# Five weight products of a four-layer graph network, by quarters in Strassen's seven products

## The reference

```python
# layer 0: x1 = x @ W1 + b1; four gate steps of _graph_gcn (tanh of two gate projections per edge)
# layer 1 (sage), twice: 
h = relu(x @ W_self0 + (agg(x) * deg_inv) @ W_neigh0 + b0)
out = h @ W_self1 + (agg(h) * deg_inv) @ W_neigh1 + b1
# layer 2 (attention): h = x @ W; e = exp(-leaky(al[src] + ar[dst])); elu(segment_sum(e * h[dst]) / rowsum)
# layer 3 (loop): relu(segment_sum((x @ W)[src] * norm) + b)
x = _layernorm(x + layer(x, ...))
```

## Time and profile before

| | us |
|---|---|
| median of three executions | 1535.95 (1535.74 to 1536.42) |
| span of the profiled execution | 1534.3 |
| TensorE busy | 1515.2 |
| VectorE busy | 883.6 |
| ScalarE busy | 753.9 |
| GpSimd busy | 187.2 |
| DMA moved | 231.75 MB, 151 GB/s on average |

### The profile page before, as it was taken

The page is one execution under the profiler, slowest core; times in us unless marked ns, Lnnn a source line. Parts: engine busy times, 40 slices in busy tenths (PEclk is TensorE's granted clock), DMA queues, the critical chain, the costliest instruction groups (busy, mean ns, idle before and its releaser), DMA issues.

```text
span 1534.3 us, 19219 instructions
## 1 busy us (share of the span) xinstructions
PE 1515.2 (99%) x6985; PEld 1220.1 (80%) x6985; DVE 883.6 (58%) x1410; ACT 753.9 (49%) x1348; POOL 187.2 (12%) x307
## 2 busy tenths in 40 slices
PE   7999999999999999999999999999999999999997
PEld 6887877878887887788878777888888778877776
DVE  9888788887545442423332353567598356436346
ACT  7677767768633342433332233345696246533233
POOL 0110021333200000000000000212053013100003
PEclk9999999999999999999999999999999999999999
DMA  6333154226764424333354424554466248545336
GB/s 200 123 122 107 47 191 132 84 78 224 261 237 149 161 96 155 119 113 116 114 171 130 143 81 166 196 203 166 147 197 190 94 143 297 182 131 171 94 121 186
DMA packets 103198, 231.75 MB, mean 151 GB/s; under 512 B 23162, under 2 KB 25972, under 8 KB 103096
## 3 DMA queue, kind: packets, MB, share of 16 engines
q1 hardware_dynamic: 90126, 191.62, 39.3%
q10 hardware_dynamic: 12970, 38.77, 6.6%
HBM read 170.98 MB, written 59.37 MB: 150 GB/s over the span
## 4 chain that ended last, share of the span: by engine, by line
PE 96%; DVE 3%; ACT 1%; issue 0%; DMA 0%; POOLq 0%; DVEq 0%; ACTq 0%
PE bank L986 18%; PE bank L842 16%; PE bank L844 15%; PE bank L843 15%; PE bank L997 9%; PE bank L990 9%; PE bank L988 9%; PE bank L1075 2%; PE bank L912 2%; PE bank L880 1%; DVE oK L1801 0%; ACT Tt L1159 0%; DVE wl L1445 0%; DVE Tt L1483 0%; DVE oL L1791 0%
## 5 line engine op out<-in xcount | busy, mean ns | idle before, releaser
L842 PE MATMUL bank<-wh,xh 128*125 128x512 f32 x1032 | 413.4, 401 | 0.9 <-ACT xh L1124 0.9
L843 PE MATMUL bank<-wl,xh 128*125 128x512 f32 x1040 | 410.3, 395 | 0.0
L844 PE MATMUL bank<-wh,xl 128*125 128x512 f32 x1040 | 409.6, 394 | 0.0
L986 PE MATMUL bank<-Zh,Mh 125*125 125x512 f32 x990 | 394.9, 399 | 0.0
L1457 DVE TENSOR_TENSOR xl<-xs,xh 128x1000 fp32r<-128x1000 f32 x130 | 155.5, 1199 | 291.0 <-ACT xh L1124 290.6
L1124 ACT CAST xh<-xs 128x1000 fp32r<-128x1000 f32 x130 | 132.9, 1026 | 303.0 <-PE bank L844 290.8
L997 PE MATMUL bank<-Zl,Mh 125*125 125x512 f32 x590 | 232.5, 394 | 0.0
L844 PEld LDWEIGHTS bank<-wh,xl 128*125 128x125 f32 x1040 | 193.0, 186 | 48.9
L843 PEld LDWEIGHTS bank<-wl,xh 128*125 128x125 f32 x1040 | 193.1, 186 | 45.4
L842 PEld LDWEIGHTS bank<-wh,xh 128*125 128x125 f32 x1032 | 191.0, 185 | 46.6 <-ACT xh L1124 1.1
L986 PEld LDWEIGHTS bank<-Zh,Mh 125*125 125x125 f32 x990 | 183.5, 185 | 44.0
(11 more groups left out here) (188 smaller groups left out, 1825.3 us busy)
## 6 DMA issues: line engine op xcount, KB each, us to landing
xs<-xT_d SPq DMA_DIRECT2D x80, 500.0 KB, 3.6
Ar<-a_d SPq DMA_DIRECT2D x100, 312.5 KB, 3.4
xs<-hT_d SPq DMA_DIRECT2D x40, 500.0 KB, 3.4
x_d<-XO ACTq DMA_DIRECT2D x30, 512.0 KB, 4.7
R<-x_d SPq DMA_DIRECT2D x60, 256.0 KB, 4.2
xT_d<-XT ACTq DMA_DIRECT2D x30, 500.0 KB, 3.8
ws<-in_W SPq DMA_DIRECT2D x30, 256.0 KB, 3.6
Tt<-m_d SPq DMA_DIRECT2D x10, 625.0 KB, 4.5
```

Source lines behind the costliest of these rows:

```text
L842: te.matmul(o, xh[i % 2][:, k, :], wh[s][:], start=(k == 0), stop=False)
L843: te.matmul(o, xh[i % 2][:, k, :], wl[s][:], start=False, stop=False)
L844: m = te.matmul(o, xl[i % 2][:, k, :], wh[s][:], start=False, stop=(k == 7))
L986: te.matmul(o, Mh[i][:, s, :], zh, start=(n == 0), stop=False)
```

## The change

The `z` and `self` products of both sage layers and the `z` product of the loop layer (`PRODUCTS`) are cut into quarters: x into upper and lower five row tiles and left and right 512 inner columns, the weights likewise. Strassen's form with seven products (in Winograd's variant, the phases P1 to P7) gives the same result. Each phase is five jobs (`HT = 5`), each job `quarter_product` with 4 slabs x 3 = 12 matmuls. 20 jobs of 24 matmuls become 35 of 12.

- Sums of x quarters (`four_sums` on VectorE, "x" steps) are made from the transposed x, for two row tiles at a time, and stored in `xs_d`; the neighbour product of the first sage layer uses those of the self product, and the second uses its own likewise. Sums of weight quarters (`four_sums` on GpSimd, "w" steps) go to `ws_d`. A step loads 1 MB into one of two places (`PW`: U3 or XO), makes four sums, each on the one before, and stores 1 MB. `sums_schedule` gives the turns: loaded one turn before, stored two turns after.
- x tiles are loaded by half (four half places, `X_SLOT`), four turns ahead. Slabs: 28 of 256 KB for a product in place of 16. Results of phases are added up in `U2`, `U3`, `U` and `G`. P2 is multiplied onto P1's bank and P3 onto P5's (`ONTO`).
- The self product now comes whole, before the neighbour product; its right half is stored (`sr_d`) and loaded again for the means. Mean jobs no longer alternate with self jobs. PSUM banks are no longer held for a partner.
- W2 steps (attention vectors times weights) move from self and z jobs to the first sixteen mean jobs. The biases get a second place.

The diff, cut to its core:

```diff
+SELF_ORDER = ("P1", "P2", "P4", "P6", "P7", "P5", "P3")
+Z_ORDER = ("P1", "P2", "P6", "P7", "P4", "P5", "P3")
+X_QUARTER = {"P1": (0, 0), "P2": (0, 1), "P4": (1, 1)}
+W_QUARTER = {"P1": (0, 0), "P2": (1, 0), "P3": (1, 1)}
+X_SUM = {"P6": 0, "P3": 1, "P7": 2, "P5": 3}
+W_SUM = {"P6": 0, "P5": 1, "P4": 2, "P7": 3}
+ONTO = {"P2": "P1", "P3": "P5"}
...
+    for layer in range(1, 5):
+        if layer < 3:
+            for p in SELF_ORDER:
+                jobs += [Job("self", i, layer=layer, phase=p, g=g) for i in range(HT)]
+                g += 4
         for f in range(2):
...
+            for p in Z_ORDER[5:] if f else Z_ORDER[:5]:
+                jobs += [Job("zq", i, layer=layer, phase=p, g=g) for i in range(HT)]
+                g += 4
+            jobs += [Job("mean" if layer < 3 else "loop", d, f, layer) for d in range(NT)]
...
+    steps = [(J0[0] + 4 + 6 * k, "w", 0, k) for k in range(4)]
+    at = {p: find(*p, phase="P1") for p in PRODUCTS}
+    steps += [(at["self", 1] + 2 * i, "x", 1, i) for i in range(HT)]
+    steps += [(at["self", 1] + 11 + 2 * k, "w", 1, k) for k in range(4)]
+    steps += [(at["zq", 1] + 2 + 3 * k, "w", 2, k) for k in range(4)]
+    steps += [(at["self", 2] + 2 * i, "x", 2, i) for i in range(HT)]
+    steps += [(at["self", 2] + 11 + 2 * k, "w", 3, k) for k in range(4)]
+    steps += [(at["zq", 2] + 2 + 3 * k, "w", 4, k) for k in range(4)]
+    steps += [(at["zq", 4] + 2 * i, "x", 4, i) for i in range(HT)]
...
+    STEP_LOAD.setdefault(_t - 1, []).append(_n)
+    STEP_AT.setdefault(_t, []).append(_n)
+    STEP_STORE.setdefault(_t + 2, []).append(_n)
...
+        PW = [U3F[:], XB[:].rearrange("p (q c) -> p q c", q=4)]
...
+            def step_load(n):
+                t, what, p, i = STEPS[n]
+                if n >= 2:
+                    step_stored(q, n - 2)
...
+                elif what == "x" and p == 1:
+                    for d in range(NT - 2, NT):
+                        q.wait_ge(s_tt, GROUPS[fin_of(0, d)][-1][0] + 1)
+                        x_stored(q, fin_of(0, d))
...
+                if what == "w":
+                    for r in range(2):
+                        sy.dma_start(dst[:, 2 * r:2 * r + 2, :], MATRIX[p][r * HW + i * 128:r * HW + (i + 1) * 128, :]
+                                     .rearrange("p (q c) -> p q c", q=2)).then_inc(d_pl[n % 2], 16)
+                    return
...
+            def step_store(n):
+                t, what, p, i = STEPS[n]
+                q.wait_ge(s_sums, n + 1)
+                if what == "w":
+                    sy.dma_start(ws_d[p][i], PW[n % 2]).then_inc(d_ps[n % 2], 16)
+                else:
+                    sy.dma_start(xs_d[p][i], PW[n % 2][:, :, 0:QX]).then_inc(d_ps[n % 2], 16)
...
+            def quarter_product(j):
...
+                for k in range(4):
...
+                    te.matmul(o, xh[b][:, 4 * h + k, :], wh[s][:], start=(k == 0 and not onto), stop=False, skip_group_check=True)
+                    te.matmul(o, xh[b][:, 4 * h + k, :], wl[s][:], start=False, stop=False, skip_group_check=True)
+                    m = te.matmul(o, xl[b][:, 4 * h + k, :], wh[s][:], start=False, stop=(k == 3), skip_group_check=True)
...
+            def four_sums(n):
+                v = PW[n % 2]
+                s11, s12, s21, s22 = (v[:, k, 0:QX] for k in range(4))
+                q.wait_ge(d_pl[n % 2], 32 * (n // 2 + 1))
+                q.wait_ge(s_sums, n)
+                chain("v", ve.tensor_tensor(s22, s21, s22, ALU.add))
+                mine()
+                chain("v", ve.tensor_tensor(s21, s11, s21, ALU.subtract))
+                mine()
+                chain("v", ve.tensor_tensor(s11, s22, s11, ALU.subtract))
+                mine()
+                ve.tensor_tensor(s12, s12, s11, ALU.subtract).then_inc(s_sums, 1)
...
+                elif job.phase == "P7":
+                    made("self", layer, i, "P6")
+                    u3_free_of_steps(q, j)
...
+                    ins = ve.tensor_tensor(U3[i], U2[i], p, ALU.add)
```

More of the change, by code:

```diff
@@ L120, in finishes @@
         return 0
-    if job.layer == 2 and job.second and job.half == 1:
+    if job.kind == "mean" and job.layer == 2 and job.half == 1:
         return 1
@@ L630, in h_of @@
         def h_of(f, d):
[L631 to L643 removed]
+            return find("mean", 1, d, f)
```

807 lines of the change are left out of this document (554 added, 253 removed).

## The result

The changed kernel takes 1686.84 us (median, 1686.39 to 1692.98) against 1536.18 beside it on the same chip: 1.0988 times the kernel before, 95% interval 1.097 to 1.1006. The profiled execution has a span of 1684.7 us. The forecast was 1513.5, with 1484 to 1551 as its range.

A forecast was written before the change was run, and what follows sets the result against it. TensorE was taken to bound the kernel, with 96% of the chain and no gaps between matmuls. 1535.95 - 69.7 for removed matmuls + 47.3 of stall (11.4 + 18.2 + 10.7 + 4 + 3) = 1513.5 us; eight in ten: 1484 to 1551.

The forecast's parts named there:

- three terms of the DMAs' rate: Stall from full DMA engines: self product of layer 2 11.4 us, self of layer 1 18.2, loop layer 10.7.
- What is removed: 69.7 us: Five products of 480 matmuls become 420 each: 300 fewer at 0.2324 us, 69.7 us if everything else stays hidden.
- Rival 4: Quarter jobs could run at a slower pace, +3% of 2100 matmuls would be 15 us; chance 0.02.
- VectorE, 0: Quarter jobs' splits, sums and four-sum steps on VectorE cost 0 to 2 us a product; taken as 0.
- ScalarE, and what only moves: ScalarE's casts, mean jobs in a row, W2 steps and right-half reloads: nothing, 1 us if the last loads are late.
- GpSimd: step 6.5, gates 3: Four dependent GpSimd sums take 6.5 us a step; four steps in the gates cost 3 us through VectorE's port.
- DMAs, rate 380: Dense traffic with the steps' loads and stores in self and loop products was taken to move at 380 GB/s.
- The bound of 338: Lower bound on the DMA rate, in GB/s: what 241 GB/s at a share of 0.71 comes to.
- SyncE's lead, 10 us: SyncE issues loads ahead of TensorE's turn; about 10 us of this lead buffers late DMAs.
- Neighbour products, 2 each: Weight steps every 8.37 us against rounds of 11.2, less 10 of lead: 2 us each, 4 in all, bounds 0 and 9.
- Rival 2: SyncE stands at stores awaiting GpSimd's sums: 20.5 us per neighbour product, 1550; sign turns at 14.1 us a round; chance 0.16.
- Rival 3, the clock: A granted clock under 1.00 was its sign; chance 0.05.

## Why the prediction was wrong, by its own steps

Of the 220.1 us of waiting the forecast had 47.3. What it missed are 60.0 us in the neighbour products, 57.0 in the three terms of the DMAs' rate, 27.3 in the mean stages, 13.6 at the end, 6.5 in the gates and 8.4 elsewhere.

- **What is removed: 69.7 us.** This step was right. 300 matmuls fewer; in every stretch without a stall five quarter jobs take 13.9 to 14.0 us, which is 0.2324 a matmul. Rival 4 is out.
- **VectorE, 0.** This one is small. Without the stores, x loads and VectorE's sums together cost 19 to 26 us, and no run divides the two.
- **ScalarE, and what only moves: "the means' wait ... nothing".** The step failed, by 22.3 us in layer 2's second half and 5.0 in layer 1's. The price was counted as busy time per job (1.7 of 2.79, VectorE with two sums). The self jobs that were taken out from between were not seen as cover: mean jobs of 4.65 us in a row stand against a ring of 9.7 us through three engines. The reload was counted as bytes; it also halves how far ahead a row can be loaded.
- **The end of the kernel.** The forecast had no term for it, and 13.6 us came, 12.9 of them also without any step. The cause is open.
- **GpSimd: step 6.5, gates 3.** The step is right: 6.5 measured. The gates cost 9.5; with weight steps alone 12.0. The term was too small by a factor of three to four; with transfers alone the gates cost nothing, so it is the additions.
- **DMAs, rate 380.** The term was mis-sized: 307 GB/s at a share of 0.97. The bound of 338 was not low enough. It had been read from the kernel before, which has none of the steps. With 307 the prediction's own formula gives 28.5 / 0.307 - 58.6 = 34.2 for layer 2's self product less 5 of lead, 29.2, measured 30.7; 26.0 / 0.307 - 50.2 = 34.5 for layer 1's, measured 41.3; 13.6 / 0.307 - 25.1 = 19.2 for the loop product, measured 25.3. So the form, with the rate put right, gives 83 of 97 us. The other 14 are not taken apart; the round of loads and stores, 9.8 us, has no place in the form.
- **SyncE's lead, 10 us.** It is worth that, but the stores of the right half take it away before it can be used: without them the two neighbour products are 11.0 and 11.1 us shorter.
- **Neighbour products, 2 each.** This is the step that failed worst: 31.2 and 32.8 where 4 in all had been put. The round was taken as landing 4.7 + sums 6.5 = 11.2; measured 1.8 + 7.2 + 6.5 = 15.5. Rival 2 had 16 us and the turning point at 14.1. With the measured round and no lead its formula gives 4 x (15.5 - 8.37) = 28.5, within 5 us of what came. It was given 0.16, on the ground that a landing takes 3.6 to 4.7; those are medians over the whole kernel before, which moves 151 GB/s on average, and the landing here had 252 GB/s beside it.
- **Rival 3, the clock.** It is there: 0.81 to 0.85 in the stalled stretches, as a mean of the levels of 1.2 and 2.4 GHz, and TensorE is busy 1518.4 us where 1515.2 - 69.7 = 1445.5 would do. In the phase right after a stall the clock is 1.00 again and a job takes 2.79. Whether the slower matmuls inside a stall add to it, or only fill what would be waiting, no run separates. The forecast took the lower level's 0.77 us a matmul from a row at 8.89 us, where the granted clock reads 1.00; but in the kernel without steps a matmul shows 0.77 us too, at 993.33, and there the clock is 0.52 (991 to 994).

The Trainium skill ("TensorE: Matmul & The Clock Gate", HAM oscillation) tells of waits for DMA that bring the clock down each time anew. The trace agrees, with 0.81 to 0.85 on the stalled stretches.

What the parts share: each term was counted as if the others kept their cover. 50 without steps, 64 and 83 with one kind, and 23 more when both are there.

## What to carry to other kernels

Before taking work out of TensorE, write down which rings through the other engines that work covers, and how long each is; jobs put in a row lose the cover that jobs in turn gave each other. An engine that issues all loads in order must not wait for a result that is made beside it: give such a step the queue of the engine that makes it, and see that this engine has nothing older to wait for. When a ring has two links, a change of one shows little: test them together before ruling either out.

## What the runs showed of the hardware that I had not expected

- DMA engines at a share of 0.97 to 0.99 moved 307 GB/s where large loads and stores are mixed, 350 at 1.01 with rows of 4000 and 8000 bytes for 2000, and 360 at 1.00 in the kernel without the x stores. A share near one is no sign of one rate. The Trainium skill ("Perfetto Trace Analysis", Roofline) lets a single core reach about 435 GB/s by its 16 engines; the three stretches here stay well below that.
- A weight step's load landed 7.2 us after its issue at a share of only 0.71, and the store of a 1 MB step took 8.5 us.
- A GpSimd sum of 128x512 took 1.28 us once and 1.60 to 1.74 in the three after it. TensorE kept its pace beside it all the same (99.6% busy in 549 to 577 of the kernel with GpSimd's own queue).
